# The order of POOL's work in the second pass: two MLP units ahead of the scaled rows and their copies

## The reference

```python
# L1
h = roll(_ln(x, g1, b1), (-3, -3))            # windows of 7 x 7
attn = softmax(q @ k.T * scale); out = (attn @ v) @ w_proj + b_proj
x = shortcut + roll(out, (3, 3))
h2 = _ln(x, g2, b2)
x = x + gelu(h2 @ w_fc1 + b_fc1) @ w_fc2 + b_fc2
# L2, its first lines
xn = (x - mu) * rsqrt(var + EPS) * norm_gamma + norm_beta
dw = depthwise_conv_7x7(roll(xn, (-3, -3)), dw_w) + dw_b
```

## Time and profile before

| | |
|---|---|
| median of 3 runs | 11228.43 us (11223.51 to 11228.84) |
| profiled execution | 11222.26 us |
| its span | 11220.5 us |
| second pass (L1) in the span | about 1806 to 5124 us |
| busy in the span: PE, DVE, ACT, POOL | 95%, 68%, 67%, 52% |
| busy in 3000 to 3500 us: PE, DVE, ACT, POOL | 478, 365, 378, 366 of 500 us |

### The profile page before, as it was taken

The page is one execution under the profiler, slowest core; times in us unless marked ns, Lnnn a source line. Parts: engine busy times, 40 slices in busy tenths (PEclk is TensorE's granted clock), DMA queues, the critical chain, the costliest instruction groups (busy, mean ns, idle before and its releaser), DMA issues. The chain is left out here.

```text
span 11220.5 us, 391982 instructions
## 1 busy us (share of the span) xinstructions
PE 10679.5 (95%) x158292; PEld 8402.3 (75%) x158292; DVE 7580.4 (68%) x13453; ACT 7550.8 (67%) x12917; POOL 5850.2 (52%) x7492
## 2 busy tenths in 40 slices
PE   6999998999999999998989999998999999999999
PEld 3666666777777777777767777776888888888887
DVE  4555555777777777774467676766777777777776
ACT  4555554777777777774357676765777777777777
POOL 2333333777777777771034444443555555555555
PEclk9999998999999999999989999998999999999999
DMA  2111111222222222225633333332111111111110
GB/s 61 51 46 49 48 43 34 52 52 52 52 52 52 52 52 52 52 53 163 216 88 79 76 80 77 79 77 55 26 26 26 26 26 25 26 26 26 26 26 23
DMA packets 1105563, 617.40 MB, mean 55 GB/s; under 512 B 864635, under 2 KB 1076550, under 8 KB 1099688
## 3 DMA queue, kind: packets, MB, share of 16 engines
q1 hardware_dynamic: 1091368, 552.46, 20.7%
q10 hardware_dynamic: 12288, 38.54, 1.0%
HBM read 307.18 MB, written 282.75 MB: 53 GB/s over the span
## 5 line engine op out<-in xcount | busy, mean ns | idle before, releaser
L1508 POOL TENSOR_TENSOR L_HdL<-L_Hd,L_HdH 128x392 fp32r<-128x392 f32 x1536 | 1578.1, 1027 | 280.9 <-POOL L_HdH L1506 230.0
L1002 PE MATMUL banks<-L_ident,L_PR 113*113 113x113 f32 x9216 | 1204.9, 267 | 1.5 <-ACT L_PR L1247 0.8
L1002 PEld LDWEIGHTS banks<-L_ident,L_PR 113*113 113x113 f32 x9216 | 1146.0, 181 | 66.0 <-DVE L_X L1412 9.7
L1231 ACT COPY L_PT<-banks 113x452 f32<-113x452 f32 x1792 | 886.0, 538 | 397.6 <-PE banks L1002 395.4
L1247 ACT ACTIVATE L_PR<-L_SX 113x588 f32<-113x588 f32 x1536 | 1087.9, 708 | 84.6 <-DVE L_SX L1369 10.1
L1065 PE MATMUL banks<-L_VB,L_PT 113*49 113x34 f32 x36864 | 1074.3, 213 | 2.0 <-ACT L_PT L1231 1.0
L1065 PEld LDWEIGHTS banks<-L_VB,L_PT 113*49 113x49 f32 x36864 | 1006.2, 126 | 63.5 <-issue 1.6
L1363 DVE TENSOR_REDUCE L_MX<-banks 113x12 f32<-113x588 f32 x1024 | 782.7, 764 | 360.9 <-PE banks L1048 360.9
L1497 POOL CAST L_XNH<-L_XN 97x392 fp32r<-97x392 f32 x512 | 448.3, 876 | 1098.9 <-DVE L_XN L1425 1098.9
L1506 POOL CAST L_HdH<-L_Hd 128x392 fp32r<-128x392 f32 x1536 | 784.0, 510 | 329.9 <-issue 305.3
L1556 POOL COPY L_XN<-L_XR 96x392 f32<-96x392 f32 x256 | 151.8, 593 | 1290.7 <-DMA L_XR<-L_norm 1207.1
(11 more groups left out here) (247 smaller groups left out, 28650.8 us busy)
## 6 DMA issues: line engine op xcount, KB each, us to landing
L_X<-after_L SPq DMA_DIRECT2D x768, 147.0 KB
after_L<-L_X SPq DMA_DIRECT2D x512, 147.0 KB
conv_T<-L_norm_by_phase SPq DMA_DIRECT2D x96, 512.0 KB, 3.3
L_norm_by_phase<-L_XP SPq DMA_DIRECT2D x512, 84.0 KB, 2.1
scan_XT<-in_x SPq DMA_DIRECT2D x32, 1176.0 KB, 7.1
L_norm<-L_XA SPq DMA_DIRECT2D x256, 147.0 KB, 1.9
L_conv<-conv_D ACTq DMA_DIRECT2D x96, 392.0 KB, 3.0
L_XR<-L_norm SPq DMA_DIRECT2D x256, 147.0 KB, 2.4
```

The source lines that it names most:

```text
L1002: mm = pe.transpose(bank(TURN[a])[0:SPAN, (k % 4) * SPAN:(k % 4 + 1) * SPAN], PR[:, st.v if lag else st.u, 2 * k:2 * k + 2, :].rearrange(" ...
L1231: act.copy(PT[:, st.v if lag else st.u, 4 * a:4 * a + 4, :].rearrange("c k q -> c (k q)"), bank(TURN[a])[0:SPAN, 0:4 * SPAN]).then_inc(s[f ...
L1508: pool.tensor_tensor(HdL[:, u, j].bitcast(F32R), Hd[:, u, j], HdH[:, u, j], ALU.subtract).then_inc(s[f"hd_parts_{j}"], 1)
```

## The change

In POOL's step the two calls that split MLP units 0 and 1 of chunk t-2 move up, from the end of the step to a place between `split_rows` and the block that makes XA and XP (`third_norm(st)`, which is true in L1 alone). Nothing is added or taken out. In L3 the block between is absent, so its order stays as it was; L2 has another POOL program.

```diff
                         if st.ahead().f:
                             split_rows(st.ahead())
+                        if st.m:
+                            split_units(st, 0, 2)
+                            split_units(st, 1, 2)
                         if third_norm(st):
 
                             c = st.t - 6
...
                                 ins = pool.tensor_copy(XP[:, st.u, ph, :, first:first + JW], pixels[:, p])
                             ins.then_inc(s["xp"], 1)
-                        if st.m:
-                            split_units(st, 0, 2)
-                            split_units(st, 1, 2)
```

## The result

The changed kernel takes 11358.9 us (median of 4 runs, 11355.6 to 11360.4), the kernel before, run beside it, 11226.0 us (4 runs, 11221.9 to 11228.8): a ratio of 1.012, 95% interval 1.0107 to 1.0133. Its profiled execution took 11360.36 us, of which the span is 11358.6, 138.1 more than the span before. All of it lies in the second pass: from the tenth SQ of the pass to the last, 246 steps take 3280.5 us in place of 3142.1, a difference of 138.4, or 0.56 us a step.

A forecast was written before the change was run, and what follows sets the result against it. TensorE's wait for POOL would go, but SyncE's queue (load of X behind the XP store) would set the second pass's step: 13.15 against 12.60 us; 245 x 0.55 = +135 us, forecast 11360 us, range 11295 to 11430.

The forecast's parts named there:

- The loop through SP's queue: Second pass: load of X behind the XP store, XP behind two units; sum 13.16 us, taken as 13.15, +0.55 a step.
- The landing of the load: Time from the load of X (L901) to POOL's SQ: taken as 3.23 us, bounds 2.95 to 3.51.
- The 19 steps of the earlier trace: Steps with the XP store issued less than 0.9 us before the load and SQ waiting: 2.95 to 3.51, mean 3.23 us.
- the floor of the earlier trace: Fourth pass, where nothing goes out just before the load: load to SQ 2.36 us.
- POOL's own loop: Second pass, output(2) through DVE, ACT and POOL back to output(2): 12.54 us; as rival -15 us, 11213, chance 0.11.
- The blocked DVE: XN2L (L1429) held up by SQ3 on POOL: ends up to 0.86 us later, step 13.40 us.
- the whole wait is won: Rival: unit 2 keeps up and TensorE's wait goes: 0.47 x 245 = -116 us, 11112, chance 0.05.

The follow-up runs named there:

- experiment 7: Changed kernel, SyncE still waiting for XP ahead of the load of X but issuing the XP store behind it: 11241.1 us, 1.0011 of the kernel before.
- experiment 1: Changed kernel, with SyncE's stores of XA and XP moved behind the next step's load of X: 11220.0 us, 0.9995 of the kernel before.
- experiment 3: Changed kernel, with SQ3 ahead of SQ in POOL's step and SyncE's queue untouched: 11255.3 us, 1.0027 of the kernel before.
- experiment 5: Kernel before, with XA and XP moved behind unit 2 at the head of POOL's step, for chunk t-5: 11050.4 us, 0.9843.
- experiment 6: Changed kernel, with only unit 0 ahead of XA and XP and unit 1 left behind them: 11289.1 us, 1.0054 of the kernel before.
- experiment 4: Changed kernel, with the two XP stores issued a second time, into a spare buffer, ahead of the load: 11744.8 us, 1.0462 of the kernel before.

## Why the prediction was right

**The loop through SP's queue** was the right mechanism, and each of its terms was near. Means over the 246 steps, from the starts of the instructions in the trace after, beside the forecast's: XNH to XA (over two units) 5.37, forecast 2.07 + 3.33 = 5.40; XA to the store 1.66, forecast 1.64; the pair to the load 1.33, forecast 1.21; load to SQ 3.25, forecast 3.23; SQ to XNH 1.72, forecast 1.68. Together they are the mean step of 13.34, against 13.16 before overlaps; the median step is 13.15, as forecast. The mean is higher than the median mostly by the turn of the loop of 24 unrolled steps: nine times, 24 steps apart, 4.1 to 5.5 us pass from the pair's start to the load in place of 1.14, and the two steps there are on average 2.4 and 1.4 us over the median. The same two are 2.6 and 1.6 over it in the trace before, whose mean is 12.77 (3142.1 / 246) against an ordinary 12.60. So the difference of the means, 0.56, is the forecast's 0.55, and 246 of it is the 138 us. The forecast worked with ordinary steps alone; that the turn costs both kernels nearly the same is nothing it had worked out, and that the total came out within 2 us, in a range of 135, is luck.

**The landing of the load** was the term with the widest bounds. The 19 steps of the earlier trace rows gave it within 0.02 us, and the floor of the earlier trace rows would have given the wrong sign. That it is the store just ahead which makes it long, the trace after shows by itself: at the turn of the loop the load goes out long after the pair, and in eight of the nine such steps SQ starts 2.35 to 2.45 us after it, as here (2.39):

```profile
2953.75 1.02 SPq L934 DMA_DIRECT2D L_norm_by_phase<-L_XP  x2
2958.07 0.79 SPq L901 DMA_DIRECT2D L_X<-after_L  x2
...
2960.46 0.84 POOL L1492 TENSOR_TENSOR L_SQ<-L_X 96x392 f32<-96x392 f32 x1 [2.76 <-DMA L_X<-after_L]
```

The Trainium skill's estimate for it (DMA: Bandwidth & Descriptors, section "Anatomy of one DMA — SWDGE (gpsimd) path"), 2.35 us, is a fit for transfers that GpSimd issues, and SP issues these. In size it agrees with the loads that have nothing of XP's just in front, 2.4 us in experiment 7 and at the turn of the loop, and not with those behind the store, 3.2: what is missing in it is the queue.

**POOL's own loop** as the next limit was right in kind: experiment 1 has it and nothing else. Its 12.54 was short by 0.05: two units took 3.38 there, not 3.33. The -15 us of that rival would have been 0; 11220.0 against 11227.4 can't be told from no change.

**The blocked DVE** (13.40) was named as an end of the range and is not what sets the usual step. XN2L does run late beside POOL, as the line's own view shows (min/median/max ns), before and then after, with XN2L of the step above:

```profile
L1429 DVE TENSOR_TENSOR L_XN2L<-L_XN,L_XN2H x235: 566/567/569, 1999.8 to 4991.2; 97x392 fp32r<-97x392 f32 x118
```

```profile
L1429 DVE TENSOR_TENSOR L_XN2L<-L_XN,L_XN2H x255: 566/1090/1667, 1857.0 to 5239.3; 97x392 fp32r<-97x392 f32 x128
```

```profile
3015.40 0.99 DVE L1429 TENSOR_TENSOR L_XN2L<-L_XN,L_XN2H 97x392 fp32r<-97x392 f32 x1
```

At the median it is twice as long, by 0.52 us, and TensorE waits for it at `hidden`, 191 times. But the steps of after are alike with and without it: 13.07 us from output(2) to output(2) (median) in the 186 in which XN2L took over 0.6 us, 13.16 in the 53 in which it did not. In either case the way to unit 0 starts from a late SQ3, and its two branches, XNH and XNL on POOL and XN2L with the GELU, end close together: unit 0 starts 0.16 us after the GELU's end (median), where 0.15 is the time it takes when it waits for the GELU alone. In experiment 1, with the same order on POOL, XN2L takes 0.57 us in every step. Where the load is late but no longer the limit the delay does cost, 0.42 and 0.46 us in the steps that have it (experiments 3 and 7). The 13.40 of the forecast had XN2L run its whole 0.57 us behind SQ3. In the step above SQ3 ends at 3015.97 and XN2L at 3016.39, 0.42 later. The Trainium skill (SBUF — State Buffer, section "Who interferes with whom") calls what the two engines share "an exclusive lock". That agrees in kind, the longest XN2L being 1.10 us over the undisturbed one, with SQ and then SQ3 beside it; in size the loss is some 0.15 us less than the wait for SQ3's end would make it.

**What was wrong** lay beside the forecast. The stall's worth was taken as its mark of idleness, 0.47 us, and is 0.70, so the rival "the whole wait is won" would have given some -178 us and not -116 (experiment 5). And the loop was drawn from output(2) alone; the 1.91 us that TensorE needs from output(1) to output(2) belong in it as well. They explain the 12.60 of before, which the forecast took as given: unit 0 to output(1) is 3016.53 - 3013.08 = 3.45, output(1) to output(2) 1.91, output(2) to XA 3011.67 - 3005.84 = 5.83, and XA and XP ahead of unit 0 3013.08 - 3011.67 = 1.41: together 12.60. XA and XP are a term of that loop, and in the two other places tried ahead of output(2) (experiments 1 and 6) they were one of the loop that took its place.

## What to carry to other kernels

A move on one engine is also a move on every queue that waits for what is moved: follow its result to the queue that sends it, and ask what stands behind that send. Here a load stood behind a store in one in-order queue, and a step in which TensorE had waited 0.47 us for POOL became 0.56 us longer. Before moving work earlier or later, draw the whole loop, through every engine and queue, and put optional work where no term of any loop passes; here that was behind the last unit, in the rest that POOL had anyway, worth 1.6%.

## What the runs showed of the hardware

A load that goes out right behind the scattered XP store lands 0.8 us later than one in front of it (3.21 in median against 2.44 us to SQ, and 2.35 to 2.45 where the store had gone out long before). By the packets in the trace after, the load's first packet follows its issue by 0.97 us either way, but the 96th of its 97 comes at 2.46 us among the store's 128-byte packets and at 1.72 without them (172 steps could be told apart). The issue of such a pair itself varies: 0.89 us in the usual step of after, 1.16 in median and 2.06 in a slow step of the kernel that issues two pairs (experiment 4). The idle mark ahead of a matrix product is less than the stall is worth: marked 0.46, the stall cost 0.70 us of step, since the starts of products are 0.80 us apart across it and 0.26 just behind it, against 0.18 in a run of them. A DVE subtraction of two SBUF tiles that starts beside a running POOL instruction on SBUF ends late: XN2L, 0.57 us undisturbed, ends 0.42 us after the SQ3 that it started beside.
